# Moving the PSUM copies of the output store from VectorE to ScalarE in an eight-core two-layer transformer kernel

## The reference

```python
# layer 0
x = _layernorm(x + _L0_attn_ref(x, ...))   # gated linear recurrence: chunked scan, two projections
x = _layernorm(x + _L0_ffn_ref(x, ...))    # quantized activations times a packed ternary weight
# layer 1
x = _layernorm(x + _L1_attn_ref(x, ...))   # 16-head attention with relative position embeddings
x = _layernorm(x + _L1_ffn_ref(x, ...))    # two layers: local attention (window 512), gated GELU FFN
return x
```

## Time and profile before

| | us |
|---|---|
| median of 2 runs | 10188.05 |
| lowest and highest run | 10160.9, 10215.2 |
| the profiled execution's own time | 10210.16 |
| its span, slowest core (7) | 10208.6 |
| fastest core (4) | 9997.9 |

### The profile page before, as it was taken

How to read it: one execution, slowest core, us unless ns; L and a number is a source line. 1 busy time by engine, 2 the same in 40 slices (tenths; PEclk the granted TensorE clock), 3 DMA queues, 4 the chain that set the end, 5 groups by cost and what they waited for, 6 DMA issues and landing times.

```text
span 10208.6 us, 60182 instructions; the slowest of 8 cores (9997.9 to 10208.6 us)
## 1 busy us (share of the span) xinstructions
PE 5245.0 (51%) x19111; PEld 2006.8 (20%) x19111; DVE 2732.1 (27%) x3977; ACT 1670.7 (16%) x3009; POOL 840.0 (8%) x813
## 2 busy tenths in 40 slices
PE   4352574555555555555555564234339843344894
PEld 2111131111111222111111121011114311111341
DVE  5746412000000000000000012633351145334314
ACT  2100011222222222222222201011101011111100
POOL 0000010000000000000000001211111112111010
PEclk7675785555555555555555576555559965556896
DMA  3000131111111111111111112000004310000331
GB/s 58 10 4 0 36 51 30 35 39 39 38 39 37 34 35 33 34 39 39 39 36 38 38 50 54 4 0 1 0 5 38 35 15 1 0 1 5 30 33 66
DMA packets 458424, 285.26 MB, mean 28 GB/s; under 512 B 307482, under 2 KB 403995, under 8 KB 454027
## 3 DMA queue, kind: packets, MB, share of 16 engines
q0 software_dynamic: 222240, 81.89, 7.1%
q1 hardware_dynamic: 180588, 120.34, 4.5%
q10 hardware_dynamic: 55296, 79.19, 2.1%
HBM read 227.39 MB, written 118.96 MB: 34 GB/s over the span
## 4 chain that ended last, share of the span: by engine, by line
PE 43%; DVE 18%; DMA 17%; ACT 11%; issue 6%; SPq 3%; DVEq 1%; POOL 1%; ACTq 1%; POOLq 0%; PEldq 0%; PEld 0%
DMA sc_amax<-amaxc 7%; PE pm L1145 5%; ACT xb L1140 5%; DMA sc_qre<-wm 4%; PE pm L1929 3%; PE pb L1950 3%; SPq L49 3%; DVE wm L974 2%; PE pm L1123 2%; PE pb L1158 2%; PE pb L1743 2%; PE pm L1995 2%; PE pb L1995 2%; ACT wm L1022 2%; PE pm L1118 2%
## 5 line engine op out<-in xcount | busy, mean ns | idle before, releaser
L974 DVE RECIPROCAL wm<-pm 1x512 f32<-1x512 f32 x64 | 214.5, 3352 | 3518.3 <-PE pm L970 3518.3
L1140 ACT ACTIVATE xb<-pm 128x512 bf16<-128x512 f32 x1024 | 611.4, 597 | 1969.6 <-PE pm L1133 1182.6
L1145 PE MATMUL pm<-xb,U 128*65 128x512 bf16 x576 | 342.8, 595 | 604.9 <-ACT xb L1140 604.9
L1708 DVE TENSOR_REDUCE amaxc<-pm 128x1 f32<-128x640 f32 (+4 forms) x256 | 181.8, 740 | 815.5 <-PE pm L1704 813.9
L49 POOL DMA_DIRECT2D wj<-sc_qre x128 | 70.5, 553 | 3726.2 <-PE pm L1128 2334.9
L1015 PE MATMUL pb<-wj 128*128 128x512 bf16 x256 | 140.1, 558 | 435.4 <-ACT wm L1022 399.6
L1754 ACT ACTIVATE xb<-pb 128x512 bf16<-128x512 f32 x448 | 243.1, 594 | 600.9 <-PE pb L1743 600.9
L1123 PE MATMUL pm<-qer,wj 128*128 128x512 bf16 (+4 forms) x576 | 308.1, 535 | 0.0
L1731 PE MATMUL pb<-wm,zbuf 1*65 1x512 bf16 x64 | 38.6, 603 | 493.4 <-DMA wj<-sc_amax 493.4
L1133 PE MATMUL pm<-wj 128*128 128x512 bf16 (+4 forms) x576 | 290.9, 505 | 0.0
L220 PE MATMUL pm<-xb,wj 128*128 128x512 bf16 x512 | 137.7, 436 | 279.6 <-ACT U L231 257.1
(11 more groups left out here) (446 smaller groups left out, 9509.8 us busy)
## 6 DMA issues: line engine op xcount, KB each, us to landing
sc_qre<-wm ACTq DMA_DIRECT2D x256, 256.0 KB, 2.0
xb<-sc_e SPq DMA_DIRECT2D x256, 128.0 KB, 2.4
wm<-l1f_w POOLq DMA_DIRECT2D x116, 256.0 KB, 4.3
sc_xspill<-xr SPq DMA_DIRECT2D x16, 1024.0 KB, 13.4
wm<-W_qkv POOLq DMA_DIRECT2D x48, 256.0 KB, 4.3
sc_e<-xb ACTq DMA_DIRECT2D x112, 96.0 KB, 2.0
sc_e<-xb SPq DMA_DIRECT2D x112, 96.0 KB, 1.9
xin<-x SPq DMA_DIRECT2D x16, 512.0 KB, 4.1
```

Of the source, the lines that this page charges most:

```text
L974: p.op("vector", lambda q, c2=ctxp: q.reciprocal(out=srow[0:1, 0:512], in_=c2[64:65, 0:512]))
L1140: q.activation(out=o, in_=i_, func=AF.Exp), s_se)
L1145: q.matmul(o, l, r, start=st, stop=False), None)
```

## The change

The 128 copies out of PSUM in the output store go from VectorE (`tensor_copy`) to ScalarE (`activation` with `AF.Copy`). ScalarE now waits for the transposes and for the stores, and gets one wait for the last vector work ahead of the loop. The last copy of a tile signals a new semaphore, `s_so`, on which SP and TensorE wait in place of `s_ve`. The drain that VectorE had ahead of each group of copies has no counterpart. The transposes, buffers, banks, sizes and stores are as before.

```diff
+    s_so = p.sem("s_so")
     s_st2 = [p.sem("s_st0"), p.sem("s_st1")]
     st_done = [0, 0]
     p.wait("tensor", s_ve, p.sems["s_ve"].n)
+    p.wait("scalar", s_ve, p.sems["s_ve"].n)
...
-            p.wait("vector", s_tr, p.sems["s_tr"].n)
+            p.wait("scalar", s_tr, p.sems["s_tr"].n)
             if st_done[buf]:
-                p.wait("vector", s_st2[buf], st_done[buf])
-            if i >= 1:
-                p.drain("vector")
+                p.wait("scalar", s_st2[buf], st_done[buf])
             for k in range(4):
                 j = half * 4 + k
-                p.op("vector", lambda q, o=yout[buf][:, 128 * j:128 * (j + 1)],
+                p.op("scalar", lambda q, o=yout[buf][:, 128 * j:128 * (j + 1)],
                      s=pm[:, bank * 512 + 128 * k: bank * 512 + 128 * (k + 1)]:
-                     q.tensor_copy(out=o, in_=s),
-                     s_ve if (half == 1 and k == 3) else None)
-        evtok = p.sems["s_ve"].n
-        p.wait("sync", s_ve, evtok)
+                     q.activation(out=o, in_=s, func=AF.Copy),
+                     s_so if (half == 1 and k == 3) else None)
+        evtok = p.sems["s_so"].n
+        p.wait("sync", s_so, evtok)
         p.dma("sync", out_y[128 * i:128 * (i + 1), :], yout[buf][:], s_st2[buf])
         st_done[buf] = s_st2[buf].n
-        p.wait("tensor", s_ve, evtok)
+        p.wait("tensor", s_so, evtok)
```

## The result

| | before | changed |
|---|---|---|
| median of the runs, us | 10216.2 (26 runs) | 10173.2 (27 runs) |
| lowest and highest run | 10095.1, 10387.6 | 9987.3, 10267.1 |
| ratio | | 0.9871, 95% interval 0.9827 to 0.9915 |
| slowest core's span in the profiled execution | 10208.6 | 10171.6 |

The comparison says 1.3% faster, with an interval clear of 1, where the prediction had 0.05%. The ratio is that of the means of the runs within 1.5% of the fastest run of the same kernel (20 before, 5 changed), while the medians in the table are over all runs and differ by 0.4%.

The account below looks back on a forecast made before the run. The slowest core 7 sets the time; its output store, 56.3 us, is a chain alternating between TensorE and VectorE. Saving 0.32 us on 16 tiles, 5.1, less 0.5 for a slow store, gives 10188.0 - 4.6 = 10183.4 us, range 10110 to 10240.

Parts of the forecast that it names:

- The stage: Output store at the kernel's end: a tile falls from 3.31 to 2.99 us, net 4.6 us saved over 16 tiles.
- no table load: ScalarE's copies after its square root need no new function table; one load would cost 1.28 us, once.
- The copies' pace: ScalarE's 128x128 copies start every 0.16 to 0.20 us; 0.16 taken, a group of four in 0.75 against 0.90 us.
- The rival of copies that do not overlap: ScalarE's eight copies per tile step above 0.21 us; with no overlap the kernel takes 8 us more, 10196; chance 0.10.
- The reading of the Trainium skill: ScalarE copies from PSUM cost 250 ns with latency exposed: tile slower by 0.2 us or so, kernel about 3 us.
- The drains: VectorE's drains vanish: 0.12 plus 0.04 us between a tile's groups, about 0.05 ahead of the first.
- The stores: Output stores, median 2.7 us, still fit; rival: they become the bound, 2 us more, 10190; stores or hiccup chance 0.12.
- The clock in the stage: TensorE's granted clock stays 0.50 in the output store; rival: it rises, 5 us more saved, 10178; chance 0.04.
- The term for the wander between runs: Whole kernel: two runs 54 us apart, 27 each way from their median, set the range; mechanisms add at most 10.
- two thirds of the way to core 3's time: Reason for the range's lower end, 10110: core 3's time lies 111 us below the median of the runs.
- the 195 us of the earlier trace: Extra wait of core 7 over core 3 at line 1731, block 3's local attention: 493.4 against 298.9 us.
- should cores 6 and 7 once wait no longer than core 3: Case of shorter waits in block 3's local attention on these cores: the kernel's time would be near 10077 us.

Follow-up runs that it names:

- the ten-fold pair: Output store looped ten times, with VectorE's copies (kernel before) and with ScalarE's (changed kernel): 10761.6 and 10693.1 us; ten stages 535.6 and 491.0 us on core 0.
- the split version: Ten output stores with one 128x512 copy per bank, VectorE then ScalarE, TensorE waiting for its own bank: 10444.7 and 10675.7 us; stage 319.5 us on core 0.
- second control: The kernel before, unchanged, run again on the chip of the kernel with row exchange and split store: 10312.4 us, ratio 0.9965.
- the two repetitions: The changed kernel run again, twice, each beside the unchanged kernel on one chip: 10244.4 and 10296.6 us, ratio 1.0004 both times.

## Why the prediction was right and where it failed

**The stage: right, step by step.** Tile 3.02 us against 2.99 forecast, stage 51.2 us in a forecast of 50.8 to 54, no table load, clock at 0.50, one wait for a store. The gain of 5.1 us on core 7 compares with 4.6 forecast; all cores together give 4.6, and the ten-fold pair 4.5.

**The copies' pace: right, at the lower bound.** A group of four takes 0.80, so the step is (0.80 - 0.28) / 3 = 0.17 us, between the bounds of 0.16 and 0.20 and near the one taken for its source in PSUM. The rival of copies that do not overlap needed more than 0.21. The reading of the Trainium skill (VectorE: DVE Perf Modes, section The TRN2 errata) by which each such copy would cost 250 ns does not hold for the step here; its estimate would have been a slower tile. What the section calls exposed between instructions is the latency of SBUF; that it holds for copies out of PSUM was the prediction's own reading.

**The drains: right in kind, a little large.** Forecast at 0.2 a tile, measured 25.4 / 160 = 0.16. They were more than half of what the change saves; moving the copies was the smaller half.

**The stores: right.** One wait, of 1.6 us; median landing 2.6 us. They become the bound only in the split version, at 2.0 us a tile.

**The clock in the stage: right for this change.** It stayed at 0.50, as forecast. In the split version it went to 0.88, which the expectation of that run had not allowed for.

**The step that failed: "the two runs are 27 us each way from their median, to which the mechanisms add at most 10".** The term for the wander between runs was far too small, and with it the range and its lower end, "two thirds of the way to core 3's time". The prediction read the 195 us of the earlier trace rows and then treated them as nearly fixed: "should cores 6 and 7 once wait no longer than core 3". They are not fixed. Call a pair late when it ends after 10080 us: in the 28 executions of the changed kernel whose cores are known, none to all four pairs are late, and three executions have no late pair: 9987, 10007 and 10072 us. The runs of the kernel before span 292 us (26 runs) and those of the changed one 280 (27 runs), not 54. With the exchange through DRAM taken out, the medians fall by 346 us and the wait with them.

The prediction also took the wait for the whole difference between cores, where its own rows say otherwise: core 7 waits 194.5 us longer than core 3 at line 1731 and ends only 131.6 later. Core 3 lost time elsewhere; its TensorE was busy 5290.4 us against 5245.0 on core 7. The second control shows what such a loss goes with: a granted clock that differs between pairs in the same stretch, and 72 us more of TensorE's busy time. So core 3's time was no floor.

**How the 0.9871 comes about as a number.** The mean of the 5 runs of the changed kernel that enter the ratio (9987.3 to 10130.9) is 10058.7, that of the 20 runs before (up to 10232.2) is 10189.8, and 10058.7 / 10189.8 = 0.9871. The comparison sets runs with no or one late pair against runs of all sorts. If three runs of 53 have no late pair and fall at random, all three fall to the changed kernel with a chance of (27 x 26 x 25) / (53 x 52 x 51) = 0.12. That none of the runs before was of this kind is read from their times (10095.1 at the lowest); their cores are known only for the profiled one.

Chance does not settle the first comparison by itself. The means over all its runs differ by 42 us with a standard error of 17, more than the 5 us of the stage. What speaks against a cause in the kernel are the two repetitions, each with both kernels on one chip: the ratios are 1.0004 twice, and the changed kernel's mean lies 7 and 5 us under that of all unchanged runs on its chip, with standard errors of 16 and 17. From one of the three comparisons to the next the same kernel moves by as much as was to be explained: the first pair of the changed kernel to be done ends at 9963, 10019 and 10090 us (medians). Whether both kernels of the first comparison ran on the same chip is not known.

What was shown: the change is worth 4.5 to 5 us in its stage; the control, unchanged, comes out at 0.9964 and 0.9965; taking the exchange away takes away the wait at line 1731 and most of the gap between pairs; a lower granted clock goes with a second part of the gap. What stays open: why a pair of cores is late, or gets a lower clock, in one execution and not in the next, and where the rest of the 42 us of the first comparison comes from. Nor can it be excluded that the changed kernel has late pairs a little less often; nothing in its code ahead of the store differs.

## What to carry to other kernels

Before pricing an edit, price the comparison: look at which cores set the time, at what wait and in what granted clock they differ, and whether that is the same from run to run; an unchanged kernel run as a control costs one run and shows how far an interval can be trusted. An effect of 5 us in 10000 is measured by multiplying the stage and reading its length in the trace, not by the time of the whole. When copies move to another engine, look for what goes with them: here a drain on which nothing in the loop depended was more than half of the gain.

## What the runs showed of the hardware

- Four stores of 512 bytes in 4-byte pieces and the load behind them held TensorE for 281 to 570 us in 64 steps. The two cores of a pair are late together (10228.6 and 10231.0, 10253.1 and 10258.5 in one execution), and the other pairs of the same execution need not be (10023.5 and 10010.4).
- In one stretch of block 3 with TensorE busy without a pause, one pair of cores was granted 0.81 and the others 0.99 to 1.00 in the same execution (second control).
- ScalarE's 128x128 float32 copies out of PSUM follow each other every 0.17 us at 284 ns each; VectorE's every 0.20 ((0.89 - 0.28) / 3, without drains).
- The granted clock of the output store was 0.50 in the kernel before and in the changed one, where TensorE stops in every tile until the last copy is done. In the split version, where it waits only for its own bank, it was 0.88 (core 0), and a 128x128 float32 transpose took 273 ns (median) instead of 421.
